# Cross-attention of a perceiver block: the context taken relative to its last token, and its two parts made on ScalarE and VectorE

## Reference

```python
x = x + cross_attention(layernorm(x), ctx, ctx)     # 16 heads of 16, softmax over the 257 tokens
x = x + self_attention(layernorm(x))                # per batch over 32 tokens, rms norm, rotary, sigmoid weights
x = x + moe(layernorm(x))                           # 8 experts, top 1, capacity 160, 256 -> 1024 -> 256

# cross_attention
q = xn @ Wq.T + bq ; k = ctx @ Wk.T + bk ; v = ctx @ Wv.T + bv
out = softmax(q k^T) v @ Wo.T + bo
```

## Time and profile before

| | |
|---|---|
| median of 3 runs | 1329.99 us (1329.96 to 1330.12) |
| the profiled execution | 1326.77 us, of which the span of the profile is 1324.9 |
| mean granted TensorE clock | 0.946 of full speed |
| busy PE / DVE / ACT / POOL | 1160.6 / 851.6 / 801.9 / 568.9 us |

### The profile page before, as it was taken

The page is one execution under the profiler, slowest core; times in us unless marked ns, Lnnn a source line. Parts: engine busy times, 40 slices in busy tenths (PEclk is TensorE's granted clock), DMA queues, the critical chain, the costliest instruction groups (busy, mean ns, idle before and its releaser), DMA issues. The chain is left out here.

```text
span 1324.9 us, 43348 instructions
## 1 busy us (share of the span) xinstructions
PE 1160.6 (88%) x17169; PEld 980.9 (74%) x17169; DVE 851.6 (64%) x2395; ACT 801.9 (61%) x2347; POOL 568.9 (43%) x1045
## 2 busy tenths in 40 slices
PE   6898988989889889999988988998999988874897
PEld 5677777777777777777777777777787777752796
DVE  4667777776776677766677766777666667653111
ACT  5677666666666666666666766766656666632121
POOL 2344444454554444445445444444444544432021
PEclk9999999998999999989999999999888999975899
DMA  6415111111111111111111111111111111000474
GB/s 156 124 46 182 54 58 54 58 57 34 52 50 54 49 36 50 51 47 52 36 47 48 50 51 31 50 50 51 46 45 36 48 50 46 14 10 13 135 227 138
DMA packets 71927, 82.32 MB, mean 62 GB/s; under 512 B 16987, under 2 KB 50732, under 8 KB 71728
## 3 DMA queue, kind: packets, MB, share of 16 engines
q1 hardware_dynamic: 65280, 75.19, 19.3%
q0 software_dynamic: 3200, 3.71, 0.8%
q10 hardware_dynamic: 3248, 0.66, 0.2%
HBM read 64.79 MB, written 16.56 MB: 61 GB/s over the span
## 5 line engine op out<-in xcount | busy, mean ns | idle before, releaser
L735 ACT ACTIVATE prob<-score,nmx 128x257 f32<-128x257 f32 x512 | 236.2, 476 | 219.1 <-DVE nmx L936 218.8
L401 PE MATMUL kps<-ctx_p,wk_p 128*128 128x256 f32 x1536 | 217.4, 292 | 0.3 <-POOL ctx_p L1235 0.2
L411 PE MATMUL vps<-wv_p,ctx_p 128*128 128x256 f32 x1536 | 214.7, 289 | 0.0
L401 PEld LDWEIGHTS kps<-ctx_p,wk_p 128*128 128x128 f32 x1536 | 200.0, 196 | 6.1 <-issue 1.9
L1235 POOL TENSOR_TENSOR ctx_p<-ctxT,ctx_p 128x512 fp32r<-128x512 f32 x128 | 152.3, 1190 | 117.1 <-ACT ctx_p L751 116.7
L411 PEld LDWEIGHTS vps<-wv_p,ctx_p 128*128 128x128 f32 x1536 | 191.5, 191 | 12.4 <-issue 12.4
L936 DVE TENSOR_REDUCE nmx<-score 128x2 f32<-128x514 f32 x256 | 165.2, 687 | 51.7 <-PE score L428 51.7
L1253 POOL TENSOR_TENSOR plast<-const,prob 128x128 f32<-128x128 f32 x128 | 64.1, 501 | 255.8 <-DVE prob L947 255.8
L947 DVE TENSOR_SCALAR prob<-prob,rsum 128x257 f32<-128x257 f32 x512 | 158.5, 352 | 9.0
L953 DVE COPY probT<-score 128x512 f32<-128x512 f32 x96 | 66.4, 691 | 126.2 <-PE score L444 125.9
L444 PE MATMUL score<-const,prob 128*128 128x128 f32 x1024 | 140.8, 281 | 2.3 <-DVE prob L947 2.1
(11 more groups left out here) (159 smaller groups left out, 2029.3 us busy)
## 6 DMA issues: line engine op xcount, KB each, us to landing
ctxT<-in_ctxT SPq DMA_DIRECT2D x128, 257.0 KB, 3.0
w<-in_w SPq DMA_DIRECT2D x16, 1024.0 KB, 8.7
xq<-in_x SPq DMA_DIRECT2D x32, 128.0 KB, 3.2
xr<-in_x SPq DMA_DIRECT2D x32, 128.0 KB, 2.1
qbd<-qkT SPq DMA_DIRECT2D x256, 16.0 KB, 1.9
out<-row SPq DMA_DIRECT2D x32, 128.0 KB, 1.9
slots<-row SPq DMA_DIRECT2D x10, 257.0 KB, 5.6
x_a<-slots SPq DMA_DIRECT2D x8, 129.0 KB, 2.1
```

The lines of the kernel that those rows point to most:

```text
L401: last = mm(kps[:, c, :], wk_p[:, x, n, c * P:(c + 1) * P], ctx_p[:, g, y, n, :], start=(n, x) == (0, LO), stop=(n, y) == (C - 1, LO))
L411: last = mm(vps[:, c, :], ctx_p[:, g, x, n, c * P:(c + 1) * P], wv_p[:, y, n, :], start=(n, x) == (0, LO), stop=(n, y) == (C - 1, LO))
L735: last = af(prob[:, m, :], score[:, m, 0:S], ACT.Exp, bias=nmx[:, m:m + 1], scale=1.0, accum_out=esum[:, m:m + 1])
```

## The change

The last token's features are negated once (`nlast`, VectorE). `context_hi` becomes two activations of 128x256 with `nlast` as bias, moved ahead of the exponentials of its batch (in j = 3 behind the copy of y2T). `context_lo` goes from GpSimd to VectorE as two operations of 128x256 that add the same scalar and subtract the high part; it stands behind the maxima (in j = 2 ahead of `evac_qk`, in j = 0 ahead of `extract`). Column 256 of `kT` is now the key bias, set once. `last_key`, `last_prob`, `last_probs`, the old `last_values` and `attended` are gone; so is the key half of `last_rows`, whose value half moves from the start to (0, 2) of the first body. The even heads are taken by VectorE in `extract`, with the last value added (it is the same for all queries of a batch); `extract` stands behind `maxima` and `context_lo`. `scores2` goes from (0, 1) to (0, 0). `positions` stays at (0, 1), with its waits. `normalise` works on 256 columns.

```diff
 # TensorE
-                    (0, 0): s1 and (lambda: (turn("att_tmp", t1 + 1), last_probs(t1))),
-                    (0, 1): lambda: (t3 is not None and positions(t3),
-                                     s2 and (turn("relu_done", t2 + 1), scores2(t2))),
-                    (0, 2): s1 and (lambda: (turn("x1_step", 3 * t1 + 1), project_out(att, wo, "att_done", t1, "o1_ps"))),
+                    (0, 0): s2 and (lambda: (turn("relu_done", t2 + 1), scores2(t2))),
+                    (0, 1): t3 is not None and (lambda: positions(t3)),
+                    (0, 2): (s1 and (lambda: (turn("x1_step", 3 * t1 + 1),
+                                              project_out(att, wo, "ext_step", 2 * t1 + 2, t1, "o1_ps")))
+                             or once(i) and (lambda: (turn("vlast_done", C), last_rows()))),
...
 # ScalarE
             def exps(t, j):
                 b = TB * t + j
-                act.wait_ge(s["plast_done"], b)
...
             def context_hi(t, j):
                 b, r, g = TB * t + j, j // 2, j % 2
+
                 act.wait_ge(ctx_in[r], 16 * C * (t + 1))
                 act.wait_ge(s["v_done"], floor0(b - 1))
-                af(ctx_p[:, g, HI, :, :], ctxT[:, r, :, g, 0:SM], ACT.Copy).then_inc(s["ctx_hi"], 1)
+                for c in range(C):
+                    last = af(ctx_p[:, g, HI, c, :], ctxT[:, r, c, g, 0:SM], ACT.Identity, bias=nlast[:, c, b:b + 1], scale=1.0)
+                last.then_inc(s["ctx_hi"], 1)
...
-                    if j == 0 and s1:
-                        act.wait_ge(s["o1_ps"], t1)
-                        even_heads(att, gather[:, :, 0, :], "pv_done", TB * (t1 + 1), "ext_step")
...
                     if j == 3 and s2:
                         copy_rows(y2T[:, :, :], sh_c, "y2t_ps", t2, "y2T_done")
+                    if xa and (j < 2 or q):
+                        context_hi(*((i, j + 2) if j < 2 else (i + 1, j - 2)))
                     if xa:
                         exps(i, j)
...
                     if ahead:
                         values(ta, ja)
-                    if xa and j < 3 and (j < 2 or q):
-                        context_hi(*((i, j + 2) if j < 2 else (i + 1, j - 2)))
...
 # VectorE
+            def context_lo(t, j):
+                b, r, g = TB * t + j, j // 2, j % 2
+                dve.wait_ge(s["ctx_hi"], b + 1)
+                for c in range(C):
+                    last = v.scalar_tensor_tensor(ctx_p[:, g, LO, c, :], ctxT[:, r, c, g, 0:SM], nlast[:, c, b:b + 1],
+                                                  ctx_p[:, g, HI, c, :].bitcast(F32), ALU.add, ALU.subtract)
+                last.then_inc(s["ctx_parts"], 1)
...
             def extract(t):
 
+                dve.wait_ge(s["pv_done"], TB * (t + 1))
+                dve.wait_ge(s["o1_ps"], t)
+                if once(t):
+                    dve.wait_ge(s["vlast_done"], C)
+                v.scalar_tensor_tensor(att[:, :, :].rearrange("p c (j q) -> p c j q", j=TB),
+                                       gather[:, :, 0, :].rearrange("p c (j q) -> p c j q", j=TB), k["even"],
+                                       vlast[:, t, :, :].unsqueeze(3).to_broadcast([P, C, TB, L]), ALU.mult, ALU.add
+                                       ).then_inc(s["ext_step"], 1)
                 dve.wait_ge(s["ext_step"], 2 * t + 1)
                 v.scalar_tensor_tensor(att[:, :, :], gather[:, :, 1, :], k["odd"], att[:, :, :], ALU.mult, ALU.add
                                        ).then_inc(s["ext_step"], 1)
...
             def body(i, half):
                 q, xa, s1, s2 = stages(i)
                 t1, t2 = i - 1, i - 2
                 for j in range(TB):
+                    if xa:
+                        maxima(i, j)
+                    if j == 1 and s1:
+                        norm1(t1)
+                    if xa and (j < 2 or q):
+                        context_lo(*((i, j + 2) if j < 2 else (i + 1, j - 2)))
                     if j == 0 and s1:
                         extract(t1)
-                    if xa:
-                        maxima(i, j)
                     if j == 0 and once(i):
                         norm_x(1)
-                    if j == 0 and s1:
-                        last_values(t1)
-                    if j == 1 and s1:
-                        norm1(t1)
                     if j == 2 and s1:
                         evac_qk(t1)
                     if xa:
                         normalise(i, j)
...
 # GpSimd
-                    if xa and (j < TB - 1 or q):
-                        last_key(*((i, j + 1) if j < TB - 1 else (i + 1, 0)))
...
-                    if xa:
-                        last_prob(i, j)
...
-                    if xa and (j < 2 or q):
-                        context_lo(*((i, j + 2) if j < 2 else (i + 1, j - 2)))
```

More of the change, by code:

```diff
@@ L365, in last_rows @@
             def last_rows():
-                pe.wait_ge(s["wk_in"], 16 * 4)
                 pe.wait_ge(s["wv_in"], 16)
-                pe.wait_ge(s["wkv_in"], 16 * 6)
+                pe.wait_ge(s["last_in"], 16)
                 for c in range(C):
                     for n in range(C):
[L372 to L377, removed]
+                        last = mm(sh_c[:, c], wv[:, n, c * P:(c + 1) * P], lastT[:, n, :], start=n == 0, stop=n == C - 1)
                 last.then_inc(s["last_ps"], 1)
@@ L463, in weighted_values, with project_out @@
                 last.then_inc(s["pv_done"], 1)
[L465 to L475, removed]
+            def project_out(x, w, ready, count, t, done):
+                pe.wait_ge(s[ready], count)
                 for c in range(C):
@@ L700, in _ @@
             load_paired(act, wk, a["Wk"], "wk_in")
-            for dst, src, done in ((wv[:], a["Wv"], "wv_in"), (lastT[:], a["lastT"], "wkv_in")):
+            for dst, src, done in ((lastT[:], a["lastT"], "last_in"), (wv[:], a["Wv"], "wv_in")):
                 act.dma_start(dst, src.rearrange("(c p) n -> p c n", c=C)).then_inc(s[done], 16)
@@ L803, in _ @@
             queries(0, 0)
-            act.wait_ge(s["wkv_in"], 16 * 6)
+            act.wait_ge(s["wkv_in"], 16 * 5)
             keys(0, 0)
-            act.wait_ge(s["last_ps"], 1)
-            for c in range(C):
-                last = af(klast[:, c, :], shared[:, c * P:(c + 1) * P], ACT.Identity, bias=b_k[:, c:c + 1], scale=1.0)
-            last.then_inc(s["klast_done"], 1)
             context_hi(0, 1)
@@ L855, in body @@
                         sigmoid_exp(t2)
-                    if xa and j == 3 and q:
-                        context_hi(i + 1, 1)
                     if j == 0 and q:
@@ L946, in normalise @@
                         m = 2 * c + g
-                        last = v.tensor_scalar(prob[:, m, :], prob[:, m, :], rsum[:, m:m + 1], None, ALU.mult)
+                        last = v.tensor_scalar(prob[:, m, 0:SM], prob[:, m, 0:SM], rsum[:, m:m + 1], None, ALU.mult)
                     last.then_inc(s["norm_done"], 1)
@@ L1100, in _ @@
             v.memset(row[:, :], 0.0).then_inc(s["slots_init"], 1)
+            dve.wait_ge(s["last_in"], 16)
+            v.tensor_scalar(nlast[:, :, :], lastT[:, :, :], -1.0, None, ALU.mult).then_inc(s["nlast_done"], 1)
             dve.wait_ge(s["wk_in"], 16 * 4)
             weight_lo(wk_p[:, LO], wk[:, :, :], wk_p[:, HI], 1)
+            context_lo(0, 0)
             dve.wait_ge(s["bq_in"], 16 * 4)
@@ L1136, in body @@
                         position(t2 - 1)
-                    if j == 0:
-                        if s1:
-                            attended(t1)
-                        if q:
-                            norm_x_apply(i + 1)
+                    if j == 0 and q:
+                        norm_x_apply(i + 1)
                     if j == 3 and s2:
@@ L1172, in body @@
                         setup(j)
+                    if j == 0 and once(i):
+                        last_values()
             tiles(body)
@@ L1316, in _ @@
             power("q", "xn_stat", 3, 0, "xn_pow")
-            context_lo(0, 0)
-            context_lo(0, 1)
-            pool.wait_ge(s["klast_done"], 1)
-            last_key(0, 0)
             def body(i, half):
```

61 lines of the change are left out of this document (18 added, 43 removed).

## The result

| | before | after |
|---|---|---|
| median | 1329.97 us (4 runs, 1326.40 to 1330.12) | 1347.30 us (4 runs, 1345.32 to 1347.83) |
| profiled execution / span | 1326.77 / 1324.9 us | 1347.65 / 1345.8 us |
| mean granted clock | 0.946 | 0.919 |

A forecast was written before the change was run, and what follows sets the result against it. TensorE, busy 88% of the span, was taken as the bound, with VectorE's order setting each tile's start. Median 1330 + 7 (lists +15, one-offs -8) + 16 for clock falls = 1353 us; range 1316 to 1372.

The forecast's parts named there:

- The chain at a tile's start: VectorE from v2 eviction through norm, maxima, context_lo and extract to the positions: maxima at 2.45, positions at 5.69 without GpSimd's delay.
- The 0.5 us for GpSimd: VectorE's context_lo at a tile's start loses 0 to 0.7 us to GpSimd's two additions; 0.5 taken.
- The wait of 1.7 to 2.2 us: TensorE's single wait at the positions per tile, in place of waits of 0.33 and 1.14 us.
- The term for the start: Tile start, bodies 3 to 31: -0.55 + 0.5 - 0.25 = -0.3 us each, 29 times, -9 us.
- the prediction's clock: Time scale at a tile's start, in us, counted from the start of VectorE's v2 eviction as zero.
- j = 2 and j = 3: context_lo ahead of the q/k eviction +0.47 us, context_hi ahead of ScalarE's exponentials +0.39; 28 bodies, +24 us.
- One-offs: Body 1 -2.9, body 2 -2.3, body 32 (pipeline drain) -2, the start of the kernel -1; together -8 us.
- the clock: TensorE drops to half clock behind the wait at the positions in one of three tiles: 10 x 1.6 = +16 us.
- rival 2: Faster: VectorE wins over GpSimd's additions and context_lo costs 0.3 a piece; 1313 to 1320 us, chance 0.28.
- Rival 1: Longer chain, but the new wait stays under what trips the clock; 1337 us, or 1330; chance 0.2.
- Rival 3: The clock falls in most tiles, 20 to 29 times, +32 to 46 us; 1369 to 1383 us, chance 0.15.
- Rival 4: scores2 waits for late transfers of the other half's keys; swallowed by the positions' wait, no time of its own, no chance given.

The follow-up runs named there:

- scores2_twice: Changed kernel with the 8 products of scores2 issued twice with the same operands; 1329.26 us (10 runs), ratio 1.0019 to the kernel before.
- before_last_sums_twice: Kernel before the change with the 4 products of last_probs issued twice with the same operands; 1325.87 us (10 runs), ratio 0.9987.

## Why the prediction came out, point by point

**The chain at a tile's start.** Right to 0.01 us at every step from the maxima to the positions. The 0.5 us for GpSimd was picked between 0 and 0.7, so that it fits to 0.01 is luck. The wait of 1.7 to 2.2 us doesn't follow from the prediction's own terms: the scores start at 0.57, with 3.22 of work behind them TensorE is ready at 3.79, which leaves 1.9 to 2.4; measured was 2.14. L1075 of before, which took up to 1.16 us in the earlier trace rows, is L1058 here:

```profile
L1058 DVE TENSOR_SCALAR pr<-ex,rse x32: 230/231/233, 108.9 to 1242.4; 128x8 f32<-128x8 f32 x32
```

`context_lo` takes 0.479 (0.475 was taken). Where it meets GpSimd's additions the pair takes 1.37 us; in j = 3, where it meets nothing, it is

```profile
743.32 0.88 DVE L913 SCALAR_TENSOR_TENSOR ctx_p<-ctxT,nlast,ctx_p 128x256 fp32r<-128x256 f32 x2 [0.54 <-ACT ctx_p L735]
```

so the meeting costs 0.49 against 0.5. The GpSimd instruction that it meets began first:

```profile
750.54 0.73 POOL L1243 TENSOR_TENSOR x1b<-x,r_o 128x256 f32<-128x256 f32 x1
...
751.24 0.92 POOL L1225 TENSOR_TENSOR xr<-xr,r_o 128x256 f32<-128x256 f32 x1
```

The pair's two instructions start at 751.06 and 751.48 and take 0.50 and 0.95 us: the first, begun 0.21 us before the end of L1243, was hardly held, and the second stood for L1225. GpSimd's second addition takes 0.92 instead of 0.73: both sides wait. That the meeting moved to the second norm (0.41 to 0.80 us), an instruction with a single input, is more than the prediction knew. The Trainium skill (SBUF — State Buffer, section Who interferes with whom) has both cases, an instruction with two SBUF inputs and one in a two-port mode, and says that the later one is blocked whole. Here the second of the pair (0.95 us) and the second norm, begun 0.07 us behind L1225, agree; which mode the norm ran in no trace shows.

**The term for the start was mis-sized.** Predicted -0.3 us a tile, measured 7.81 to 7.10, -0.71, and 0.08 more behind it. The projection follows the values after 755.17 - 753.66 = 1.51 us where the earlier trace rows have 1.94: -0.43, where only the wait of 0.25 was counted. And the values start at 6.24 on the prediction's clock, 0.05 behind the positions instead of 0.2: -0.2 against the -0.04 that was forecast. The other 0.08 of the 0.71 is the start of the scores, 0.65 behind the eviction of v2 where it was 0.57 before.

**j = 2 and j = 3.** Forecast +0.47 and +0.39; measured +0.44 (8.45 to 8.89) and +0.48 (6.87 to 7.35), and each vanishes when its one part is moved. In tiles with a long fall the cost of j = 2 is hidden, 10.51 before and 10.48 after: TensorE at half clock is later there than VectorE.

**The sum.** Lists: 28 x (35.89 - 35.77) = +3.4 us, where +15 was forecast. One-offs, from the spans: up to the first projection 53.17 to 49.95, the next two tiles 68.76 to 67.33, the last interval 34.79 to 30.94, the drain and the experts 145.3 to 147.4, together -6.4 against -8. Clock: before 10 x 1.16 + 5 x 1.90 = 21.1 us, after 12 x 1.27 + 11 x 1.77 + 5 x 2.12 = 45.3, so +24.2 against +16. Sum +21.2; the spans differ by 20.9. The forecast of 1353 against 1347 is 6 us off: the lists are 12 us lower than forecast, the clock 8 and the one-offs 2 higher, and the medians differ by 17.3 us where the spans differ by 20.9. That it came so near is in part luck, since the two large errors have opposite signs.

**The step that failed in its place is the clock.** "It can trip the clock in none of the 29 tiles or in all"; "I take one in three", right behind the positions. There it tripped in 5 of 28 tiles (6 of the prediction's 29 bodies), which at 0.85 us each (38.01 - 37.16) are 4 us. The other 20 us are 13 more tiles that fall behind the small products of `self_values`, a place that the prediction did not look at, though before it already cost 21 us. The Trainium skill (TensorE: Matmul & The Clock Gate, section HAM oscillation — how this bites in real kernels) describes a kernel that is throttled anew in each turn of its loop because each turn has a wait for data; this trace agrees on the recurrence, 28 of 28 tiles, but the fall stands behind 128 tiny products with TensorE busy in 1.61 of 2.60 us, not behind a wait for data.

**The rivals.** The forecast's "positions let in at 5.7 to 6.2" held, with 6.19, so rival 2 (faster) did not come: VectorE lost the meeting in its tile and `context_lo` cost 0.479. Rival 1, the chain without the clock, is what `scores2_twice` comes near to: no fall behind the positions, 1329 us. Rival 3, a fall in most tiles, did come in number, though at the other place, but 15 of those falls stood in the kernel before, so it cost 24 us and not 32 to 46. Rival 4 came in two tiles (L499 for a DMA, 1.0 us), and was swallowed as said.

**What stays open.** Why all 28 tiles of the changed kernel fall at `self_values` and only 15 of before. It is not the length of the wait at the positions (2.1, 1.4, 0.5 us: 28, 22, 23 tiles) nor that work was taken out ahead (`before_last_sums_twice`, which has more work there, falls in 18). Shorter tiles fall less (35.1 us: 13 or 14 falls in 28 tiles; 34.8: 11; 33.7: 10), each counted in one execution. That it hangs on when in a tile the small products come is only argued.

## What to carry to other kernels

Ask of work that is to be removed what it stands ahead of: TensorE's 0.92 us per tile stood ahead of a wait for VectorE; doubled they cost nothing, and so nothing was to be had by taking them out. An operation that frees a buffer belongs ahead of one that is needed two batches later: `extract` ahead of `context_lo` alone took 4% off, more than the whole change cost, over half of it by falls that no longer came. What shall run beside GpSimd's additions is best an instruction that isn't held up: `extract`, from PSUM, took 0.47 and 0.48 us beside them as without, the second half of `context_lo` 0.94 instead of 0.48. And where TensorE's clock falls in some repeats of a loop, sort the repeats by their falls before comparing two kernels, since an edit of the order moves the number of falls, and that can outweigh or hide what it does to the lists.

## What was not expected of the hardware

- Adding work made the kernel faster: 1 us more of matmuls in each tile, 1347 to 1329 us, because the clock fell in 22 of 28 tiles instead of 28, and in none a second time.
- Half clock came behind 128 products of 32x32 by 17 columns that kept TensorE busy in 1.61 of 2.60 us, without a wait on any semaphore; with 32 of them it did not come in any of 28 tiles.
- Waits of 2.1 to 2.2 us at the same place were followed by half clock in 5 of 28 tiles and not in the others (12 and 13 of 28 in two variants), so a wait of one length has no one price.
- An instruction of VectorE on 8 columns (L1075 of before) was held up by 0.93 us by a GpSimd operation, one on 256 columns by 0.39 us, the second of a pair on 256 columns by 0.46 to 0.47 us. GpSimd's operation had 1.14, 0.66 and 0.66 to 0.67 us to go as they began, so the price was what it had still to do less 0.20 to 0.27 us, whatever VectorE's own work; begun 0.21 us before its end, an instruction lost 0.02 us.
